# State-space stage: output projection as three float32r products, step-size products split up, third projection moved

## What is computed

```python
zxbcdt = u @ W_in                       # 256 -> 512 (z), 768 (xBC), 8 (dt)
dt = softplus(dt + dt_bias);  A = -exp(A_log)
xBC = silu(causal 4-tap convolution of xBC + conv_b)
x, Bm, Cm = split(xBC)                  # 512, 128, 128
y = _ssd(x * dt, A * dt, Bm, Cm)        # scan over rows, in chunks
y = (y - mean) * rsqrt(var + 1e-5) * norm_w
y = y * silu(z)
return y @ W_out                        # 512 -> 256
```

## Time and profile before

| | us |
|---|---|
| median of 3 executions | 2684.77 (2672.98 to 2690.03) |
| profiled execution | 2685.53 |
| its span | 2683.6 |
| state-space stage in the span | about 2168 to 2604 |
| a batch of it in the steady part | 51.2 |
| TensorE busy in the whole span | 2319.4 (86%) |
| VectorE busy | 1604.1 (60%) |
| ScalarE busy | 1372.6 (51%) |
| GpSimd busy | 1160.5 (43%) |

### The profile page before, as it was taken

How to read it: one execution, slowest core, us unless ns; L and a number is a source line. 1 busy time by engine, 2 the same in 40 slices (tenths; PEclk the granted TensorE clock), 3 DMA queues, 4 the chain that set the end, 5 groups by cost and what they waited for, 6 DMA issues and landing times. The chain is left out here.

```text
span 2683.6 us, 54555 instructions
## 1 busy us (share of the span) xinstructions
PE 2319.4 (86%) x20176; PEld 1630.2 (61%) x20176; DVE 1604.1 (60%) x4098; ACT 1372.6 (51%) x2116; POOL 1160.5 (43%) x1183
## 2 busy tenths in 40 slices
PE   7967777777999888989889987999899879999979
PEld 4545555555666555555555554666566767777768
DVE  5657777776113477777767762433444447777853
ACT  4532222222332287877888885532311457777753
POOL 4429999991001177557756752000265103223220
PEclk9979999988999899999999999999999989999999
DMA  5464445541000111211121211000000100000001
GB/s 177 137 185 136 143 143 150 162 129 60 21 1 28 40 56 52 66 52 57 49 62 53 63 41 49 0 1 0 1 0 1 38 1 1 1 1 1 1 1 64
DMA packets 158730, 148.97 MB, mean 56 GB/s; under 512 B 21440, under 2 KB 141376, under 8 KB 155392
## 3 DMA queue, kind: packets, MB, share of 16 engines
q1 hardware_dynamic: 138704, 105.51, 13.4%
q0 software_dynamic: 3456, 23.07, 2.6%
q10 hardware_dynamic: 16304, 16.83, 2.1%
HBM read 100.51 MB, written 40.63 MB: 53 GB/s over the span
## 5 line engine op out<-in xcount | busy, mean ns | idle before, releaser
L1641 POOL TENSOR_SCALAR a_dist<-a_dist,a_mq 128x512 f32<-128x512 f32 x512 | 355.6, 714 | 120.0 <-ACT a_mq L1580 120.0
L1684 DVE TENSOR_SCALAR_CACHE_REDUCE a_dist<-a_ring 128x512 f32<-128x512 f32 x512 | 331.9, 686 | 89.1 <-PE a_ring L1329 87.5
L1570 ACT ACTIVATE a_pT<-a_psT 128x1024 f32<-128x1024 f32 x256 | 258.0, 1023 | 95.4 <-PE a_psT L1341 87.8
L1341 PE MATMUL a_psT<-ident,a_dist 128*128 128x128 f32 x2048 | 266.2, 277 | 17.9 <-ACT a_pT L1570 17.8
L1341 PEld LDWEIGHTS a_psT<-ident,a_dist 128*128 128x128 f32 x2048 | 235.2, 143 | 49.7 <-ACT a_pT L1570 20.1
L1564 ACT ACTIVATE a_dist<-a_dist 128x2048 f32<-128x2048 f32 x128 | 236.9, 1902 | 42.1 <-DVE a_dist L1684 39.2
L1329 PE MATMUL a_ring<-a_stack 102*128 102x512 bf16 x512 | 183.4, 396 | 57.5 <-DVE a_dist L1684 33.3
L1329 PEld LDWEIGHTS a_ring<-a_stack 102*128 102x128 bf16 x512 | 47.5, 98 | 227.6 <-DVE a_dist L1684 162.9
L1007 POOL TENSOR_TENSOR c_y<-c_prod 128x1024 f32<-128x1024 f32 x16 | 37.2, 2346 | 310.9 <-DVE c_prod L1040 308.9
L3187 ACT ACTIVATE ds_wtm<-ds_wg,ds_par 128x256 f32<-128x256 f32 x64 | 29.1, 502 | 268.3 <-DVE ds_wg L3317 264.4
L1354 PE MATMUL a_psO<-a_pT,a_va 128*32 128x512 f32 x1024 | 137.5, 614 | 2.3 <-ACT a_pT L1570 2.3
(11 more groups left out here) (431 smaller groups left out, 5734.8 us busy)
## 6 DMA issues: line engine op xcount, KB each, us to landing
a_stack<-a_parts_dram SPq DMA_DIRECT2D x384, 64.0 KB
a_parts_dram<-a_parts SPq DMA_DIRECT2D x32, 384.0 KB, 2.5
bf_w<-in_up_w_dram POOLq DMA_DIRECT2D x10, 1024.0 KB
bf_w<-in_down_w_dram POOLq DMA_DIRECT2D x10, 1024.0 KB
ds_nbg<-tok_nbk ACTq DMA_DIRECT2D x128, 64.0 KB
feat_v<-di_part SPq DMA_DIRECT2D x16, 256.0 KB, 2.6
tok_nbk<-di_nbk SPq DMA_DIRECT2D x16, 256.0 KB, 3.0
feat_k<-di_part SPq DMA_DIRECT2D x16, 256.0 KB, 3.4
```

The source lines that it names most:

```text
L1341: last = turn(psT[:, u % 2, kb, q * P:(q + 1) * P], dist[:, g % 2, i, q, k * P:(k + 1) * P], core.ident[:])
L1570: a(pT[:, u // 2, u % 2], psT[:, u % 2], ACT.Exp).then_inc(exp_done, 1)
L1641: last = nc.gpsimd.tensor_scalar(d, d, -1.0, mq[:, g % 2, i, q:q + 1], ALU.mult, ALU.add)
L1684: ts(dist[:, gg % 2, i, q, :], ps[:], 1e-12, 3.0e38, ALU.max, ALU.min, accum_out=mq[:, gg % 2, i, q:q + 1]).then_inc(ring_out, 1)
```

## The change

The output projection gets the form of the input projection: `wout` is kept as `wout_h` and `wout_l`, and the gated, turned rows as `yT_h` and `yT_l`. Out(j) becomes 4 x 3 float32r products of 128x256. ScalarE's copy now writes `yT_h`; a new VectorE instruction per tile, `rest_of_gated`, writes `yT_l` = psX - yT_h. TensorE's next `turn_gated` and out(j) wait for `yl_done`, which that instruction gives.

The scaling of `wout` by the norm weight moves from VectorE in the stage to GpSimd in `split`, beside the splitting of the input weights, and the splitting of `wout` joins it there.

`project_dt` takes the tile as an argument and counts `dt_ps` per tile. In the tail its four parts stand as two, p6, two. In `front` they stand behind p0 to p3, and `sum_dt` stands behind p7 instead of p5. Projection p2 moves from the start of chunk 1 to chunk 0, between the state product and `yd`.

```diff
@@ split @@
         nc.gpsimd.tensor_copy(self.win_h[:], self.win[:]).then_inc(self.split_step, 1)
+        for k in range(KI):
+            nc.gpsimd.tensor_scalar(self.wout[:, k, :], self.wout[:, k, :], self.nw[:, k:k + 1], None,
+                                    ALU.mult).then_inc(self.split_step, 1)
         pool.wait_ge(self.split_step, 1)
         nc.gpsimd.tensor_tensor(self.win_l[:], self.win[:], plain(self.win_h[:]), ALU.subtract).then_inc(
             self.split_step, 1)
+        pool.wait_ge(self.split_step, KI + 2)
+        nc.gpsimd.tensor_copy(self.wout_h[:], self.wout[:]).then_inc(self.split_step, 1)
+        pool.wait_ge(self.split_step, KI + 3)
+        nc.gpsimd.tensor_tensor(self.wout_l[:], self.wout[:], plain(self.wout_h[:]), ALU.subtract).then_inc(
+            self.split_step, 1)
@@ TensorE, front @@
-                pe.wait_ge(xl_done, KD)
-                project_dt(0)
-                for p in range(NCT):
+                for p in range(NP_):
                     project(0, 0, p)
-                sum_dt(0, 0)
-                for p in range(NCT, NP_):
-                    project(0, 0, p)
+                    if p < TPB:
+                        project_dt(0, p)
+                    if p == NCT + 1:
+                        sum_dt(0, 0)
@@ TensorE, chunks @@
                     if more and c == 0:
                         project(b + 1, 1 - u, 0)
                         project(b + 1, 1 - u, 1)
-                    if more and c == 1:
-                        project(b + 1, 1 - u, 2)
...
                         nc.tensor.matmul(psX[:], b_tok[:, c % 2, :], xdec[:, c % 2, :],
                                          start=True, stop=True).then_inc(st_ps, 1)
+                    if more and c == 0:
+                        project(b + 1, 1 - u, 2)
                     pe.wait_ge(m_done, at(TPB, c + 1))
@@ TensorE, tail @@
                     pe.wait_ge(yz_done, at(TPB, j + 1))
                     if b or j:
-                        pe.wait_ge(yT_done, at(TPB, j))
+                        pe.wait_ge(yl_done, at(TPB, j))
...
                 turn_gated(0)
                 if more:
                     pe.wait_ge(yo_done, at(TPB - 1, TPB - 1))
-                    project_dt(b + 1)
+                    project_dt(b + 1, 0)
+                    project_dt(b + 1, 1)
+                    project(b + 1, 1 - u, NCT)
+                    project_dt(b + 1, 2)
+                    project_dt(b + 1, 3)
                 turn_gated(1)
                 for j in range(TPB):
                     if j >= 2:
                         turn_gated(j)
-                    if more:
+                    if more and j:
                         project(b + 1, 1 - u, NCT + j)
                         if j == 2:
                             sum_dt(b + 1, 1 - u)
-                    pe.wait_ge(yT_done, at(TPB, j + 1))
+                    pe.wait_ge(yl_done, at(TPB, j + 1))
                     if b or j:
                         pe.wait_ge(x_done, at(TPB, j))
-                    else:
-                        pe.wait_ge(scaled, KI)
                     for k in range(KI):
-                        last = nc.tensor.matmul(psG[:, 0:D], yT[:, j % 2, k, :], wout[:, k, :],
-                                                start=(k == 0), stop=(k == KI - 1))
+                        pairs = in_parts(yT_h[:, j % 2, k, :], yT_l[:, j % 2, k, :], wout_h[:, k, :], wout_l[:, k, :])
+                        for n, (lhsT, rhs) in enumerate(pairs):
+                            last = nc.tensor.matmul(psG[:, 0:D], lhsT, rhs, start=(k == 0 and n == 0),
+                                                    stop=(k == KI - 1 and n == 2))
@@ ScalarE, take_gated @@
-                    a(yT[:, j % 2], psX[:].rearrange("p (k q) -> p k q", k=KI), ACT.Identity).then_inc(yT_done, 1)
+                    a(yT_h[:, j % 2], psX[:].rearrange("p (k q) -> p k q", k=KI), ACT.Identity).then_inc(yh_done, 1)
@@ VectorE @@
-            for k in range(KI):
-                ts(wout[:, k, :], wout[:, k, :], nw[:, k:k + 1], None, ALU.mult).then_inc(scaled, 1)
...
-                dve.wait_ge(dt_ps, b + 1)
+                dve.wait_ge(dt_ps, TPB * (b + 1))
...
                 if more:
                     dt_biased(b + 1, 1 - u)
+                def rest_of_gated(j):
+                    dve.wait_ge(yh_done, at(TPB, j + 1))
+                    tt(yT_l[:, j % 2], psX[:].rearrange("p (k q) -> p k q", k=KI), plain(yT_h[:, j % 2]),
+                       ALU.subtract).then_inc(yl_done, 1)
+
+                rest_of_gated(0)
                 dve.wait_ge(yroot_done, at(1, 1))
...
                 for j in range(TPB):
                     t = at(TPB, j)
+                    if j:
+                        rest_of_gated(j)
                     if more and j < 3:
                         convolve(b + 1, 1 - u, 3 + j)
```

More of the change, by code:

```diff
@@ L1879, in __init__ @@
         self.wout = sb("sw_wout", [P, KI, D])
+        self.wout_h = sb("sw_wout_h", [P, KI, D], dtype=F32R)
+        self.wout_l = sb("sw_wout_l", [P, KI, D], dtype=F32R)
         self.cw = sb("sw_cw", [P, NCT, TAPS])
@@ L1934, in state_space_stage @@
         yr = sbf("yr", [P, TPB])
-        yT = sbf("yT", [P, 2, KI, P])
+        yT_h = core.sbuf(f"{tag}_yT_h", [P, 2, KI, P], ctx, F32R)
+        yT_l = core.sbuf(f"{tag}_yT_l", [P, 2, KI, P], ctx, F32R)
         psP = core.psum(f"{tag}_psP", [P, 2, 512], ctx)
@@ L1995, in project, with project_dt @@
                 last.then_inc(p_ps, 1)
[L1997 to L2005, removed]
+            def project_dt(b, j):
+                for k in range(KD):
+                    q, c = slice(j * P, (j + 1) * P), slice(WIN - HM, WIN)
+                    pairs = in_parts(xT_h[:, k, q], xT_l[:, k, q], win_h[:, k, c], win_l[:, k, c])
+                    for n, (lhsT, rhs) in enumerate(pairs):
+                        last = nc.tensor.matmul(psO[:, j * HM:(j + 1) * HM], lhsT, rhs,
+                                                start=(k == 0 and n == 0), stop=(k == KD - 1 and n == 2))
                 last.then_inc(dt_ps, 1)
```

8 lines of the change are left out of this document (4 added, 4 removed).

## The result

The changed kernel takes 2723.6 us (median of 4 executions, 2711.8 to 2726.7) against 2681.5 for the kernel before on the same chip. The ratio is **1.014, 95% interval 1.011 to 1.017**: it is slower, by 28 to 46 us. The forecast was 2709 with a range up to 2725. The profiled execution took 2725.19 us, its span is 2723.2, beside 2685.53 and 2683.6 before.

A forecast was written before the change was run, and what follows sets the result against it. TensorE was taken to bound the tail, with a new serial chain through VectorE leaving it idle. 7 x (2.1 + 0.8) + 3.5 = 23.8 us on 2685.5 gave 2709, range 2688 to 2725.

The forecast's parts named there:

- My own case: Whole kernel: the new chain delays each batch, the clock never, sometimes or always falls; 2704 to 2716 us, chance 0.75.
- the rival with products of 0.21 us: Output projection: weight load not hidden, so a 256-column product costs 0.21 us or more; 2725 us, chance 0.12.
- Out(j): Output projection of each tile: twelve float32r products at 0.13 us each, 1.5 us, a gain of about 0.2.
- The serial chain: Batch tail: step-size products, `dt_biased`, `yT_l`(0), turn, softplus, `dt_decay`, `yT_l`(1), out(1) in series; batch 2.1 us longer.
- VectorE's free time: Batch tail: VectorE has 2.5 us of pauses, waiting for out(0) and out(2), and receives 2.8 us of copies.
- The first rival: Batch tail: TensorE stays the bound because copies come in time; 2666 to 2674 us, chance 0.13.
- The clock: Batch tail: avoided at p6, the low level returns after TensorE's pauses in half the batches; 0.8 us a batch, ends 0 and 1.7.
- p2: Chunks: its work goes into TensorE's 1.2 us pause at `yd`, but later waits grow; 0, bounds -1.2 and +0.3.
- Front: Start of the stage: step-size products moved between projections, 2.7 us of products; 0, bounds -1.5 and +1.5.
- GpSimd: `wout` scaling, copy and subtraction, each at most 2.3 us, 7 us in a hole of 60, covered by the mixture stage.
- Last batch: Last tail, without softplus: out(0) starts 2.2 us later, three further tiles take 0.4 or 0.5 more each; +3.5 together.

The follow-up runs named there:

- The hinge runs: Changed kernel with one VectorE move each: `dt_decay` behind the second addition, 2705.0 us beside 2695.2; `yT_l`(0) ahead of `dt_biased`, ratio 1.009.
- the order mended: Changed kernel with `wout` scalings behind GpSimd's input-weight subtraction, `dt_decay` behind the second addition, `yT_l`(0) ahead of `dt_biased`: 2683.1 us, ratio 1.001.
- the split alone: Kernel before, float32 output projection, with only the tail's step-size products split as 12, p6, 12: 2685.9 us beside 2682.5.

## Why the prediction came out as it did

The time was inside the range, at its upper edge, and some 15 us above the likeliest figure. That it is inside is in part luck. My own case ended at 2716; the range reached to 2725 for the rival with products of 0.21 us, which the trace rejects. I had given 0.55 to a time within 1% and 0.40 to "slower", and it was slower. Step by step:

- **Out(j): right.** 1.49 us, forecast 1.5; 0.117 a product, forecast 0.13. The rival with 0.21 or more falls: each product has new weights, and at the high clock none is 0.21 apart. The Trainium skill, in "TensorE: Matmul & The Clock Gate", Part 3, "The mechanism", lists weight loads as overlapping only where the row group differs, but the same section also lets a load into a background weight buffer go ahead of running products. The trace disagrees with the first and fits the second: the spacing is 256 columns at 2.4 GHz, 0.107, and 0.01.
- **The serial chain: right in place and size.** Waits of 1.19 and 2.61 us were forecast as 1.2 and 2.6. With 69.57 taken off, `turn_gated(1)` begins at 2345.30 (forecast 2345.3), `dt_decay` at 2349.94 (2349.9), out(1) at 2351.34 (2351.3). The shortest batches last 53.2, 2.0 above 51.2; forecast 2.1. The hinge runs show two links by taking them away.
- **VectorE's free time: misread.** The first rival has "2.5 us of pauses in the tail", from out(0) and out(2). There is a third, for out(3), and it is the longest:

```profile
2358.67 0.48 DVE L2399 SCALAR_TENSOR_TENSOR X<-s_psG,s_yr,X 128x256 f32<-128x256 f32 x1 [2.32 <-PE s_psG L2117]
```

  With it VectorE had 4.9 us of pauses for 2.8 of copies. There was room; in the changed kernel the order kept the copies out of it, and with the order mended the batch fell to 50.6.
- **The clock: right in the mean, in part by luck.** At p6 it stayed high (2410.81 to 2412.28, 1.47 us), as forecast. It fell in the tails of five of the six batches: three times around out(0) and p7, where the pause behind hides it, and twice at out(1) or later. The extra over 53.2 was 0.4, 0.5, 0, 2.5, 0, 1.3: mean 0.8, forecast 0.8. The forecast had half of the batches at 1.7; a third of them had 2.5 and 1.3. The first 0.4 is not the clock's in the tail, where it stayed at 1.00; the first batch is 0.4 longer with the order mended, too (51.0 against 50.6).
- **p2: right**, 0 in the run with p2 alone.
- **Front: the step that failed.** "All that is moved are 24 x 0.112 = 2.7 us of products; I take 0, bounds -1.5 and +1.5." It was +4.1. The bounds priced the moved instructions and left out that the whole front runs at half clock until the clock rises, at an instant that other edits shift: the same instructions took 38.2 and 43.4.
- **GpSimd: failed in its cover.** "7 us in a hole of 60" is true of GpSimd, by chance: of the three parts, "each at most 2.3", the copy took 1.04, the subtraction 2.36 and the scalings 3.63. But the question was whom its instructions block. The scalings stood ahead of an existing subtraction of 5.65 us and pushed it onto a VectorE instruction on the path: +1.8, and the front's share above with it.
- **Last batch: right mechanism, too small.** Forecast +3.5, measured +7.2, or +7.8 with the 0.6 us counted in the line above it. The start of out(0) is as forecast, +2.2: 1.22 us behind the start of `yT_l`(0), where before it began 1.03 us ahead of the reciprocal. At full clock a tile takes 3.54 (2608.74 to 2612.28 in the mended kernel) against 3.09 before, +0.45 as forecast. Missing was the clock. In the changed kernel's last tail:

```profile
2627.00:2632.00 5.00, 3.30 (x16) 3.01 (x16) 1.50 (x3) 0.00 (x0) 0.00 (x0) 0.50 0.02 3
2632.00:2637.00 5.00, 3.59 (x17) 3.19 (x16) 1.60 (x3) 0.60 (x1) 0.00 (x0) 0.50 0.00 0
```

  It is at 0.50 from out(0) to the turn behind out(2). An out(j) takes 2.73 instead of 1.49 there, and a whole tile 5.19 (out(1) at 2629.05, out(2) at 2634.24) instead of 3.54. Before, in the same place, the clock was 1.00. I had let the clock fall in the steady tail, where TensorE pauses for 3.8 of 21 us, and not in the last, where it pauses for a third of the time.

The two missed terms (front and GpSimd, 5.9), the last tail's 3.7 and the seventh batch's 1.3, less 0.6 in the six batches, are 10.3 us. The median is 14.3 above the forecast, the profiled execution 15.9, of which 5.5 arose ahead of the mixture stage. The remaining 4 to 5.5 us are within the spread of the executions.

## What to carry to other kernels

A new instruction on an engine that has idle time is only free if nothing that it waits for, and nothing that it stands behind, is itself late: here 2.8 us of copies a batch cost next to nothing in one order (50.6, against 50.5 with the split alone) and 2 us and more in another. Write down the order on the engine that receives the work, and put the instruction that others wait for ahead of those that wait. Work given to GpSimd must be looked at from VectorE's side, and before pauses are put into TensorE's order one should know which stretches would run at the low clock.

## What the runs showed of the hardware

- Float32r products of 128x128 by 256 columns with new weights each time start every 0.117 us at the high clock, 0.21 at the low; three of them (0.35) replace one float32 product of 0.43 us.
- A VectorE product of 128x32 lasted 5.07 us instead of 0.19 while GpSimd subtracted, and 1.20 where it met only the end of the subtraction. Both times it ended 0.05 us behind it.
- The pattern of the granted clock over a stage came back in a second profile of the same kernel, batch by batch, with lengths equal to 0.1 us, though the stage began 15 us later in the trace. An edit well ahead of the stage changed it.
- In one kernel TensorE, busy without pause from its first projection on, stayed at 0.50 for some 15 us, in another with the same instructions for 3. In the first the clock had fallen 0.2 us behind the start of the stage, in the second 1.4 us ahead of it. Both were in the same pause of TensorE.
